# Second attention: every value product moves the columns of three heads instead of one

## What is computed

```python
m_new = max(f_log + m, i_t)
C_new = exp(f_log + m - m_new) * C + exp(i_t - m_new) * outer(k_t, v_t)
n_new = exp(f_log + m - m_new) * n + exp(i_t - m_new) * k_t
h = (qs @ C_new) / (max(abs(qs . n_new), exp(-m_new)) + EPS)
```

## Time and profile before

| What | us |
|---|---|
| median of 3 runs (969.29 to 970.13) | 969.85 |
| time of the profiled execution | 971.69 |
| its span, first to last instruction | 969.5 |
| TensorE products busy, in the span | 837.5 |
| VectorE busy, in the span | 668.5 |
| mean granted TensorE clock | 0.916 |

### The profile page before, as it was taken

The page is one execution under the profiler, slowest core; times in us unless marked ns, Lnnn a source line. Parts: engine busy times, 40 slices in busy tenths (PEclk is TensorE's granted clock), DMA queues, the critical chain, the costliest instruction groups (busy, mean ns, idle before and its releaser), DMA issues. The chain is left out here.

```text
span 969.5 us, 18748 instructions
## 1 busy us (share of the span) xinstructions
PE 837.5 (86%) x6718; PEld 702.1 (72%) x6718; DVE 668.5 (69%) x1501; ACT 389.0 (40%) x764; POOL 394.3 (41%) x548
## 2 busy tenths in 40 slices
PE   5889999998778968778898869899989999999994
PEld 4667777677557857667776758688878888788883
DVE  6657767677358644898565566577898775867876
ACT  2244444444542353333343344355556554222220
POOL 3123323333522237777776561756664221100001
PEclk9899999999889988999999976677898988999998
DMA  7002112200000057999940352211110000000001
GB/s 260 2 2 99 56 45 99 100 12 13 13 11 0 23 154 224 292 285 305 301 139 2 88 162 65 71 39 48 33 54 27 0 1 1 1 0 22 23 1 43
DMA packets 51385, 75.57 MB, mean 78 GB/s; under 512 B 9810, under 2 KB 43869, under 8 KB 51176
## 3 DMA queue, kind: packets, MB, share of 16 engines
q1 hardware_dynamic: 27624, 43.01, 13.6%
q0 software_dynamic: 9856, 18.92, 7.0%
q10 hardware_dynamic: 13824, 12.59, 3.8%
HBM read 70.27 MB, written 31.46 MB: 105 GB/s over the span
## 5 line engine op out<-in xcount | busy, mean ns | idle before, releaser
L537 POOL DMA_INDIRECT work<-xnd,rows_at x128 | 132.8, 1037 | 49.6 <-issue 42.9
L454 POOL TENSOR_SCALAR veps<-mv 128x2 f32<-128x2 f32 (+1 forms) x63 | 15.5, 246 | 284.3 <-DVE mv L1574 284.1
L463 POOL TENSOR_SCALAR_AFFINE_SELECT work<-work 128x256 f32<-128x256 f32 x128 | 53.5, 442 | 118.9 <-ACT work L659 118.8
L2013 DVE TENSOR_TENSOR work<-work,S 64x256 f32<-64x256 f32 x128 | 54.2, 424 | 55.6 <-ACT work L811 53.7
L972 PE MATMUL ZO<-parts 128*128 128x256 f32 x224 | 71.1, 318 | 16.1 <-DVE parts L1613 6.0
L972 PE MATMUL S<-xr,parts 128*128 128x512 f32 x192 | 83.0, 432 | 0.8 <-issue 0.8
L791 ACT ACTIVATE work<-S 128x512 f32<-128x512 f32 x64 | 38.2, 597 | 101.0 <-PE S L1311 97.0
L974 PE MATMUL S<-xr,parts 128*128 128x512 f32 x192 | 76.9, 401 | 0.0
L973 PE MATMUL S<-xr,parts 128*128 128x512 f32 x192 | 76.8, 400 | 0.0
L659 ACT ACTIVATE work<-S 128x768 f32<-128x768 f32 x64 | 51.7, 811 | 53.9 <-PE S L1046 53.9
L1311 PE MATMUL S<-ident,work 128*128 128x128 f32 x256 | 43.3, 293 | 28.8 <-DMA work<-xnd,rows_at 27.9
(11 more groups left out here) (331 smaller groups left out, 2337.0 us busy)
## 6 DMA issues: line engine op xcount, KB each, us to landing
yd<-work ACTq DMA_DIRECT2D x128, 128.0 KB
raw<-in_experts SPq DMA_DIRECT2D x74, 192.0 KB
work<-in_experts SPq DMA_DIRECT2D x36, 192.0 KB
lg_all<-in_experts SPq DMA_DIRECT2D x18, 192.0 KB
xnd<-attn_w SPq DMA_DIRECT2D x8, 256.0 KB, 2.1
shd<-work SPq DMA_DIRECT2D x8, 256.0 KB, 2.4
work<-xnd,rows_at POOLq DMA_INDIRECT x128
raw<-in_ffn SPq DMA_DIRECT2D x2, 1024.0 KB, 6.3
```

Source lines behind the costliest of these rows:

```text
L463: last = pool.affine_select(out=diagonal, in_=diagonal, compare_op=ALU.is_ge, fill=0.0, base=0, pattern=[[0, 2], [1, P]], channel_multipli ...
L537: pool.indirect_dma_start(xg[:, i % RING, b, :], None, xnd[:], bass.IndirectOffsetOnAxis(ap=rows_at[:, k:k + 1], axis=0), bounds_check=NT ...
L2013: last = dve.tensor_tensor(hx[64 * half:64 * half + 64, i % 2, :], sgx[64:128, i % 2, :], S[2 + i % 2][64:128, 0:256], ALU.mult)
```

## The change

`values1` passes to each product the 99 columns of three heads, h to h + 2, instead of the 33 of its own, and lets it write 99 columns of the bank. Only the first 33 of them are meant: the others are columns of heads h + 1 and h + 2, multiplied with the wrong head's weights. They land in columns that the products of those heads write later from new (`start=True`), in the order of the code. For heads 6 and 7 the surplus falls behind column 263, into columns that nothing reads; so `v1` has room for two more heads, which keep the ones that POOL wrote. The number of products, of weight loads and of waits stays, and no instruction changes its place on any engine. POOL's one fill of `v1` goes from 528 to 660 columns, and ACT's copy names the same 512 columns in another form.

```diff
--- before.py
+++ after.py
@@ -34,6 +34,7 @@
 EW = 3 * P
 BW = 2 * KC * P + D
 NI = 8
+WIDE = 3
 STEPS = NUNIT * NI
 CAP = 15.0
 NEG = -3.0e38
@@ -258,7 +259,7 @@
         view([P, 2, D])
         view([P, KC, T])
         view([P, 2, D])
-        v1 = view([P, 2, H1, DV1 + 1])
+        v1 = view([P, 2, H1 + WIDE - 1, DV1 + 1])
         eo = view([P, 2, D])
         gi = view([H1, T])
         gf = view([H1, T])
@@ -839,8 +840,8 @@
 
             def value_copies1(b):
                 act.wait_ge(s["c_vog"], b + 1)
-                act.activation(v1[:, :, :, 0:DV1].rearrange("p t h e -> p (t h) e"),
-                               S[2][:].rearrange("p (h e) -> p h e", e=DV1), ACT.Copy).then_inc(s["c_v"], 1)
+                act.activation(v1[:, :, 0:H1, 0:DV1], S[2][:].rearrange("p (t h e) -> p t h e", t=2, e=DV1), ACT.Copy
+                               ).then_inc(s["c_v"], 1)
 
                 act.activation(og, halves(S[3]), ACT.Exp, scale=-1.0).then_inc(s["c_oe"], 1)
 
@@ -1439,11 +1440,12 @@
 
             def values1(b, h):
                 pe.wait_ge(s["c_w"], b * H1 + h + 1)
-                o = h * (DV1 + 1)
+                cols = slice(h * (DV1 + 1), (h + WIDE) * (DV1 + 1))
                 w = wt[h % 4]
-                pe.matmul(Z[:, o:o + 33], w[:, 0:128], v1[:, 0, h, :], start=True, stop=True)
-                pe.matmul(O[:, o:o + 33], w[:, 128:256], v1[:, 0, h, :], start=True, stop=False)
-                return pe.matmul(O[:, o:o + 33], w[:, 256:384], v1[:, 1, h, :], start=False, stop=True)
+                rows = [v1[:, t, h:h + WIDE, :].rearrange("p h e -> p (h e)") for t in range(2)]
+                pe.matmul(Z[:, cols], w[:, 0:128], rows[0], start=True, stop=True, skip_group_check=True)
+                pe.matmul(O[:, cols], w[:, 128:256], rows[0], start=True, stop=False, skip_group_check=True)
+                return pe.matmul(O[:, cols], w[:, 256:384], rows[1], start=False, stop=True, skip_group_check=True)
 
             def final_input_transposes(b):
                 pe.wait_ge(s["c_xn4"], b + 1)
```

## The result

The changed kernel takes 954.12 us (median of 4 runs, 952.22 to 956.45), the kernel before beside it 969.57 us (965.22 to 970.13). The ratio is 0.985, 95% interval 0.981 to 0.989: faster. In a second measurement it was 952.33 against 969.11 us, ratio 0.982 (0.978 to 0.986). The forecast was 956.5 in a range of 946 to 969, so both lie inside it. The profiled execution took 956.45 us, its span 954.3, at the upper end of its runs.

A forecast was written before the change was run, and what follows sets the result against it. TensorE's clock, 0.80 in the second attention, was taken as the limit, with thin value products helping to lower it. Block gains of 13.5 us less 0.2 for ends gave 13.3, from 969.85 to 956.5 us, range 946 to 969.

The forecast's parts named there:

- The products cost nothing: Value products: 99 columns stream in at most 87 ns, under the 113 ns step set by the weight load; cost nothing.
- The clock rises: Second attention, 573 to 807 us: mean granted clock rises from 0.80 to about 0.90 as falls are avoided.
- block 0: First block of the second attention: 2.0 us gained of at most 3.6, because VectorE is close behind.
- block 7: Last block's output projection and the stretch from 797 to 807.2 us: 3.0 us gained of 6.9.
- blocks 3 to 5: Last thirds of these blocks: falls avoided behind value groups, gaining 1.5, 0.9 and 0.9 us.
- The sum: Gains of all blocks, 13.5 us, less 0.2 for the ends of the last products: 13.3 us.
- The load does not hide the columns: Rival, value products: each record's step is load plus stream, 11 to 22 us slower, 981 to 992 us; chance 0.06.
- The clock falls with waits, whatever the columns: Rival, second attention: no wait is removed, so time stays at 969.85 us plus at most 0.46; chance 0.10.
- VectorE takes the gain: Rival: falls vanish, last thirds of blocks 0, 1 and 7 stay as long, blocks 2 to 5 give 6.8; 963.2 us; chance 0.22.
- The chain ahead of the stage should stay as it is: Sign to check: the chain up to 573 us, before the second attention, should not change.

The follow-up runs named there:

- before_again: The kernel before, unchanged with 33 columns for each product, profiled a second time; 970.82 us in its one run.
- wide6: Changed kernel's layout with up to six heads, 198 columns, for each product instead of 99; 954.98 us, ratio 0.984 to the kernel before.

## Why the prediction was right, step by step

- **The products cost nothing.** Right. The step is 112 ns at 99 columns and the median duration 275 ns. The small part I left out is the first two records of a group, 0.06 us a group, so at most 1.9 us in 32 groups.
- **The clock rises.** Right in kind: 0.81 over the stage became 0.94 in one execution and 0.89 in another, where I named about 0.90.
- **Its size, by blocks.** The times are from one block's first queries to the next one's (L1395, now L1396, into S), in us, in two profiles of each kernel; the gain is that of their means.

| Blocks | before | changed | gain | I took |
|---|---|---|---|---|
| 0 | 28.7, 28.7 | 21.8, 27.4 | 4.1 | 2.0 |
| 1 | 39.7, 39.6 | 36.7, 38.6 | 2.0 | 2.0 |
| 2 | 30.2, 28.6 | 28.3, 26.0 | 2.2 | 3.5 |
| 3 to 5 | 83.3, 81.9 | 80.6, 82.8 | 0.9 | 3.3 |
| 6 | 22.7, 22.7 | 23.4, 22.7 | -0.3 | -0.3 |
| 7, to the feed-forward layer | 24.8, 24.9 | 20.2, 21.8 | 3.9 | 3.0 with the next row |
| the rest | 167.0, 166.9 | 164.8, 164.7 | 2.2 | |

The terms set too small are **block 0** and **block 7**. Of block 0 I had set 3.6 us as the most, and in the first profile that stretch alone gave 17.42 - 11.22 = 6.2. I had called all of VectorE's busy time there a bound, 13.4 us; but part of that work is not ahead of TensorE's. The sums of the experts' rows (3.6 us) lay within the stretch before and end 1.4 us behind it after. Block 7 and the first products of the feed-forward layer, which ran at the lower level before, gave 6.1 of the 6.9 us that I had as their most, and I took 3.0. The term set too large is that of **blocks 3 to 5**: I took what a last third had over its time at full clock for gain, but these blocks take 81 to 83 us at every clock from 0.87 (`before_again`) to 1.00 (`wide6`).

- **The sum.** 13.3 us forecast; the medians moved by 15.5 and by 16.8 us in the two measurements. That it came so near is in part luck: the terms that were too small and those that were too large largely cancel.
- **The load does not hide the columns.** Refuted by the step at 66, 99, 132 and 198 columns.
- **The clock falls with waits, whatever the columns.** Refuted by the steps from 33 to 66 to 99 columns with the same waits in the code, and by TensorE's idle time, which rose from 14.6 to 21.8 us while the clock rose. Waits still matter beside the columns: block 4's fall came behind one of 2.52 us.
- **VectorE takes the gain.** Right that something else takes over, wrong where. The rival had blocks 0, 1 and 7 stay and blocks 2 to 5 give 6.8 us. It was mostly the other way round: these four gave 3.1, and blocks 0, 1 and 7 with the rest 12.2. In blocks 3 to 5 it is not VectorE alone: at full clock the chain there goes through VectorE, POOL and transfers (`wide6`). What shortens that loop was not tried.
- **The chain ahead of the stage should stay as it is.** It did not, in the profiled execution; it varies without the change.

## What to carry to other kernels

Where a product moves few columns and each record has a floor that they don't fill, here 112 ns up to 132 columns, more columns cost next to nothing, and surplus ones can pay through the clock, here 15 to 17 us of 970, if their results fall where later products overwrite them or nobody reads. Look for it where the granted clock is low and TensorE shows as busy all the same. Count the gain only where TensorE holds the chain: blocks 3 to 5 kept their time at full clock. Stop at the width at which the stream becomes longer than the floor. Products added to fill the gaps pay for their own steps: they cost 6 and 10 us on the kernel before and gained nothing on the changed one.

## What was not expected of the hardware

- Load and stream overlap in the same rows: 111 to 113 ns a record from 33 to 132 columns, 167 at 198.
- An engine that is busy for all of a stretch can stand at half its clock, and one that idles at full clock: before, 17.42 of 17.42 us busy at 0.55 in block 0; after, 10.57 of 11.22 at 1.00 for the same work.
- Where the clock falls differs from one execution of a program to the next: the changed kernel's stage took 210.9 us at 0.94 and 219.3 at 0.89. One profile of such a stage is not its mean, and the medians of several runs were needed to size the change.
